# Mixture-of-experts rows planned in halves of 64: mixed blocks in two column tiles, 36 blocks for 39, and the block plan on GpSimd

## The chip, the cores and the metric

The kernel runs on one core of a Trainium2 chip. The metric is the device time of one execution in microseconds (us); lower is better. Engines are named as the profile names them: PE (TensorE, with PEld for its weight loads), DVE (VectorE), ACT (ScalarE), POOL (GpSimd) and SP (SyncE, which here only issues transfers; SPq and POOLq are the transfer queues of SP and POOL).

## What is computed

One pre-norm transformer layer on x of shape (8, 256, 256), so 2048 tokens of width 256. First comes linear attention, then a mixture of experts: each token goes to its top 2 of 8 experts, and a shared expert takes all tokens.

```python
x = x + attention(layernorm(x))          # phi(q) * cumsum(phi(k) * v), then Wo
h = layernorm(x).reshape(2048, 256)
top_logits, top_indices = top_k(h @ router_w, 2)
scores = softmax(top_logits)
for e in range(8):                       # rows of expert e only
    g, u = split(permuted @ w1[e], 2)    # 256 -> 2 x 512
    out_e = (silu(g) * u) @ w2[e]        # 512 -> 256
shared = (silu(h @ w_gate) * (h @ w_up)) @ w_down
x = x + sum(out * scores) + shared
```

The 4096 (token, expert) rows are routed by the data, so how many rows each expert has is known only while the kernel runs.

## The kernel before

Products are made in float16 with a high and a low part, as three products (high by high, low by high, high by low). Two stages follow one another:

1. **Dense stage** (steps `i` of 256 tokens): attention, router and shared expert. Meanwhile SP streams the experts' weights into `stage`, ACT makes their high part (`expert_hi`, line 935) and DVE their low part (`expert_lo`, line 1265) in `we` and `wd`. POOL computes small normalisation terms and writes each token's row, by indirect transfers, to its slot in the DRAM tensor `x_rows` (`to_rows`, line 512), where each expert has its own region of `CAP` rows.
2. **Routed stage** (blocks `b` of 128 rows of one expert). With P = 128 the number of blocks must hold for any routing: NBLK = (4096 + 8 * 127) // 128 = 39, though the data may need fewer. For block `b`, SP loads and transposes its rows (`load_rows`, lines 370 and 371) into `xg` and `meta`, PE makes gate and up (`expert_up`, banks bG and bU), ACT the silu (line 908), DVE `ab` (line 1209), ACT the high part (line 1052), DVE the low part (line 1483). PE transposes the high part (`turn_high`, line 782, bank bK), SP the low part (`turn_low`, line 379), and PE makes the down product (`expert_down`, bank bV or bQ). ACT scales it (line 1067) and POOL adds it to the output with an indirect transfer (`scatter`, line 574). The order on PE is up half 0 of `b`, `turn_high(b-1)`, up half 1 of `b`, `expert_down(b-2)`.

Between the stages stands the **block plan** (lines 1432 to 1475, on DVE): from the counts per expert it works out `blk_expert` (the expert of each block) and `blk_row` (its first row in `x_rows`). PE and SP read these into registers. Both wait for the semaphore `bexp_done`. On PE that wait stands in front of the last piece of the shared expert:

```python
pe.wait_ge(S["bexp_done"], 1)
load_expert(0)
down(B - 1, 3)
pe.wait_ge(S["ex_lo"], 3 * E)
```

Every engine works through its own list in the written order. A chain of dependent instructions on DVE is written with a helper `then`, which raises a semaphore and waits for it. A scatter waits for the one before it when the expert changes (`hold_i`), and always for the one two before. The results lie in four buffers `ya`, so ACT's result of block b waits for the scatter of block b-4.

Of the kernel before, what the change touches and what calls it, by code (L numbers as in the profile page):

```python
# [22 lines left out]
I32 = mybir.dt.int32  # L23
# [9 lines left out]
def layer_kernel(nc, x, w_att, w_bias, w_bo, w_shared, w_expert, out):  # L33
# [12 lines left out]
    NBLK = (2 * NT * P + E * (P - 1)) // P  # L46
    NBP = NBLK + 1
# [13 lines left out]
    with ExitStack() as ctx:  # L61
# [23 lines left out]
        def router_w(w):  # L85
# [75 lines left out]
        count, nblk, bend = sb("count", [P, E]), sb("nblk", [P, E]), sb("bend", [P, E])  # L161
        cnt_i, blk_i = sb("cnt_i", [P, E], I32), sb("blk_i", [P, E], I32)
# [3 lines left out]
        by_blk = [plan[:, n * NBP:(n + 1) * NBP] for n in range(2 * E, 2 * E + 9)]  # L166
        bexp, bexp_c, boff, boff_c, last, past, pad_f, sign, score = by_blk
# [16 lines left out]
        ya = [xn[1 - n // 2][:, n % 2, :] for n in range(NY)]  # L184
# [11 lines left out]
            rt end_done padded bexp_done pad_done  # L196
            xg_in0 xg_in1 xg_in2 xg_in3 sign_done score_done dst_done ta_ps ath_done atl_in0 atl_in1 atl_in2 o_ps y_done hold_done scattered0 scattered1""".split()
# [71 lines left out]
        def down_bank(i):  # L269
            return bT if i == B - 1 else bD  # L270

# [9 lines left out]
        def _(sp):  # L281
# [81 lines left out]
            def load_rows(b):  # L363

                if b >= NX:
                    sp.wait_ge(S["u_ps"], NP * B + b - NX + 1)
                sp.reg_load(row_reg, blk_row[0:1, b:b + 1])
                at = sp.snap(row_reg, min_val=0, max_val=E * CAP)
                src = xrows[bass.ds(at, P), :]
                sp.dma_start_transpose(xg[b % NX], src[:, 0:2 * D].bitcast(F16)).then_inc(S[f"xg_in{b % NX}"], 16)  # L370
                sp.dma_start(meta[:, b, :], src[:, 2 * D:2 * D + 8]).then_inc(S[f"xg_in{b % NX}"], 16)
# [9 lines left out]
            sp.wait_ge(S["bexp_done"], 1)  # L381
# [14 lines left out]
            sp.wait_ge(S["scattered0"], 16 * (NBLK // 2 + 1))  # L396
            sp.wait_ge(S["scattered1"], 16 * (NBLK // 2))

        @block.gpsimd
        def _(pool):  # L400
# [15 lines left out]
            pool.iota(row_i[:], pattern=[[0, 1]], base=0, channel_multiplier=1).then_inc(S["const_pool"], 1)  # L416

# [105 lines left out]
            pool.wait_ge(S["const_pool"], 10)  # L523
# [4 lines left out]
            pool.wait_ge(S["float_done"], 4)  # L528
            pool.tensor_copy(taken[0][:, 0, 0, :], base_i[:]).then_inc(S["taken_done"], 1)
# [28 lines left out]

            hold_reg = pool.alloc_register("hold_reg")

            def scatter(b):
# [4 lines left out]
                if b in (1, 2):  # L566
                    pool.wait_ge(before, 16)
                elif b >= 3:
# [4 lines left out]
                pool.nop(nofuse=True)  # L573
                pool.indirect_dma_start(out_rows, bass.IndirectOffsetOnAxis(ap=dst_row[:, b:b + 1], axis=0),  # L574
                                        ya[b % NY], None, bounds_check=NT * P - 1, oob_is_err=False,
                                        compute_op=ALU.add).then_inc(S[f"scattered{b % 2}"], 16)
# [7 lines left out]
        def _(pe):  # L584
# [200 lines left out]
            def expert_up(b, e, half):  # L785

                dst, done, free = ((bG, "g_ps", "sg_done"), (bU, "u_ps", "a_done"))[half]
                if half == 0:
                    pe.wait_ge(S[f"xg_in{b % NX}"], 32 * (b // NX + 1))
                pe.wait_ge(S[free], NP * B + b)  # L790
                w = [we[:, lo, bass.ds(e, 1), :].rearrange("p o (k h n) -> p (o k) h n", k=KC, h=2) for lo in range(2)]
                x2 = xg[b % NX]
                product(pe, dst[:], lambda k: x2[:, k, :], lambda k: x2[:, KC + k, :],
                        lambda k: w[0][:, k, half, :], lambda k: w[1][:, k, half, :], KC).then_inc(S[done], 1)

            def expert_down(b, e):

                n = b % NA
                pe.wait_ge(S["ath_done"], b + 1)
# [736 lines left out]
```

## Time and profile before

| | us |
|---|---|
| median of 3 runs | 391.04 |
| lowest, highest | 389.70, 391.97 |
| the profiled execution | 391.15 |
| its span on the core | 389.4 |
| PE, DVE, ACT, POOL busy | 349.4, 232.8, 219.8, 158.4 |
| first routed block starts on PE | 213.64 |

The span is the time from the first to the last instruction that the profile records; 1.75 us of the execution lie around it. The busy times are sums over both stages. A number such as L210 is a line of the kernel; the helper that writes most matmuls has line 210, so its groups are told apart by bank (bG, bU, bV).

### The profile page before, as it was taken

The page shows a single profiled execution, that of the slowest core. Times are in us where ns is not written, and L with a number is a line of the kernel's source. Part 1 is how long each engine was busy: PE and PEld are TensorE (multiplying, and loading weights), DVE is VectorE, ACT ScalarE, POOL GpSimd, SP SyncE. Part 2 cuts the span into 40 slices and gives each one's busy share as a digit, 9 for nine tenths or more (in the row PEclk, how much of TensorE's full clock was granted, in tenths as well). Part 3 has the DMA queues.
Part 4 walks back from the last instruction along what each step waited for, and adds up shares of the span by engine and source line. Part 5 has one row for each costly group of instructions (what it writes and reads, how often), then busy time and mean ns, then how long its engine had stood idle before and what let it go on. Part 6 is the DMA issues. An engine that isn't in the chain of part 4 may idle for free.

```text
span 389.4 us, 9032 instructions
## 1 busy us (share of the span) xinstructions
PE 349.4 (90%) x2850; PEld 261.0 (67%) x2850; DVE 232.8 (60%) x564; ACT 219.8 (56%) x397; POOL 158.4 (41%) x228
## 2 busy tenths in 40 slices
PE   6967499879899898996999999999999999999961
PEld 5756387768788787885988456666666666666640
DVE  5889967667698786866779633344344343443420
ACT  3778638667586786855536444544554455455430
POOL 4723175456474554344040033433433434334341
PEclk9899799989999999999999999999999999999997
DMA  6965242265573653726556467866686768657530
GB/s 200 381 164 191 42 98 83 56 135 169 112 235 72 141 176 90 213 69 186 183 185 137 110 92 101 94 93 98 96 96 88 107 89 100 97 86 91 72 33 0
DMA packets 81756, 47.35 MB, mean 122 GB/s; under 512 B 65328, under 2 KB 76848, under 8 KB 81328
## 3 DMA queue, kind: packets, MB, share of 16 engines
q1 hardware_dynamic: 72384, 36.08, 39.5%
q0 software_dynamic: 9328, 10.69, 17.8%
q8 instruction: 26, 0.43, 0.5%
q14 instruction: 18, 0.15, 0.1%
HBM read 19.10 MB, written 12.83 MB: 82 GB/s over the span
## 4 chain that ended last, share of the span: by engine, by line
PE 57%; DVE 14%; POOL 9%; issue 7%; ACT 5%; DMA 3%; SPq 1%; POOLq 1%; DVEq 0%; ACTq 0%
PE bU L210 16%; PE bG L210 15%; PE bV L210 9%; PE bQ L210 7%; PE bD L210 3%; DMA we<-in_w_shared 3%; PE bT L210 2%; PE bK L782 2%; PE bK L210 2%; POOL x_rows L512 2%; DVE ab L1209 2%; DVE al L1214 2%; DVE st L1086 2%; POOL y L452 2%; ACT xn L893 1%
## 5 line engine op out<-in xcount | busy, mean ns | idle before, releaser
L574 POOL DMA_INDIRECT out_y<-xn,dst_row x39 | 60.6, 1554 | 122.7 <-DVE dst_row L1491 66.3
L1209 DVE SCALAR_TENSOR_TENSOR ab<-bU,sg 128x512 f32<-128x512 f32 x67 | 46.2, 689 | 78.1 <-PE bU L210 78.1
L908 ACT ACTIVATE sg<-bG 128x512 f32<-128x512 f32 x67 | 39.7, 593 | 43.1 <-PE bG L210 43.0
L210 PE MATMUL bG<-we,work 128*128 x234 | 56.9, 379 | 0.2
L210 PE MATMUL bU<-we,work 128*128 x234 | 56.9, 379 | 0.0
L1052 ACT ACTIVATE ws_h<-ab 128x512 f16<-128x512 f32 x39 | 24.6, 630 | 49.1 <-DVE ab L1209 49.1
L512 POOL DMA_INDIRECT x_rows<-rows,slot_u x32 | 34.9, 1089 | 35.2 <-DVE rows L1157 16.0
L1483 DVE TENSOR_TENSOR ws_h<-ab,ws_h 128x512 f16<-128x512 f32 x39 | 27.0, 692 | 22.4 <-ACT ws_h L1052 22.4
L210 PEld LDWEIGHTS bG<-we,work 128*128 128x128 f16 x234 | 22.9, 98 | 20.5 <-issue 1.4
L1214 DVE TENSOR_TENSOR al<-ab,ah 128x512 f16<-128x512 f32 x32 | 22.0, 688 | 21.5 <-ACT ah L915 21.4
L210 PEld LDWEIGHTS bU<-we,work 128*128 128x128 f16 x234 | 21.4, 98 | 18.5
L210 PE MATMUL bV<-wd,ws_l 128*128 x240 | 29.6, 273 | 3.7 <-issue 3.4
L915 ACT ACTIVATE ah<-ab 128x512 f16<-128x512 f32 x32 | 20.0, 625 | 22.1 <-DVE ab L1209 21.6
L210 PE MATMUL bD<-ws_h,ah 128*128 128x256 f16 x112 | 21.4, 273 | 11.7 <-DVE al L1214 10.6
L210 PE MATMUL bG<-xT,ws_h 128*128 128x256 f16 x160 | 28.2, 280 | 3.0 <-DVE ws_l L1271 2.8
L210 PEld LDWEIGHTS bV<-wd,ws_l 128*128 128x128 f16 x240 | 23.2, 98 | 11.3 <-issue 4.9
L210 PE MATMUL bU<-xT,ws_h 128*128 128x256 f16 x160 | 27.6, 275 | 0.6 <-DVE ab L1209 0.6
L210 PE MATMUL bQ<-wd,ws_l 128*128 x228 | 28.0, 273 | 0.0
L210 PEld LDWEIGHTS bQ<-wd,ws_l 128*128 128x128 f16 x228 | 22.2, 98 | 6.5
L1059 ACT ACTIVATE ws_l<-bK 128x512 f16<-128x512 f32 x39 | 23.1, 591 | 0.1
L210 PE MATMUL bD<-ws_l,ah 128*128 128x256 f16 x112 | 21.6, 275 | 0.0
L210 PE MATMUL bD<-ws_h,al 128*128 128x256 f16 x112 | 21.4, 272 | 0.0
(227 smaller groups left out, 732.1 us busy)
## 6 DMA issues: line engine op xcount, KB each, us to landing
stage<-in_w_expert SPq DMA_DIRECT2D x24, 512.0 KB, 4.5
we<-in_w_shared SPq DMA_DIRECT2D x3, 1024.0 KB, 12.4
xs<-bo POOLq DMA_DIRECT2D x8, 256.0 KB, 3.9
out_y<-xs SPq DMA_DIRECT2D x8, 256.0 KB, 2.3
xs<-in_x SPq DMA_DIRECT2D x1, 1280.0 KB, 18.1
x_rows<-we SPq DMA_DIRECT2D x9, 134.0 KB
xs<-in_x SPq DMA_DIRECT2D x3, 256.0 KB, 4.0
work<-x_rows SPq DMA_TRANSPOSE x39, 3.0
```

The lines of the kernel that those rows point to most:

```text
L210: ins = pe.matmul(dst, a(c), b(c), start=first and s == 0 and c == 0, stop=last and s == 2 and c == n - 1, skip_group_check=lone)
L452: pool.tensor_tensor(y0[1][:], ve[1][:], minus_half[:], ALU.pow).then_inc(S["pow2"], 1)
L512: pool.indirect_dma_start(xrows, bass.IndirectOffsetOnAxis(ap=slot_u[q][:, k, t:t + 1], axis=0), rows2[q][:, t, :].bitcast(U16), None).the ...
L574: pool.indirect_dma_start(out_rows, bass.IndirectOffsetOnAxis(ap=dst_row[:, b:b + 1], axis=0), ya[b % NY], None, bounds_check=NT * P - 1, ...
L782: ins = pe.matmul(bK[:, c * P:(c + 1) * P], ar_h[b % NA][:, c * P:(c + 1) * P], ident16[:], start=True, stop=True)
L908: act.activation(sg[q][:], src[:], ACT.Silu, scale=1.0 / WS).then_inc(S["sg_done"], 1)
L915: act.activation(ah[f][:], ab[f % 2][:], ACT.Copy).then_inc(S["ah_done"], 1)
L1052: act.activation(ar_h[n], ab[b % 2][:], ACT.Copy).then_inc(S["ah_done"], 1)
L1059: act.activation(aT_h[n].rearrange("p c l -> p (c l)"), bK[:], ACT.Copy).then_inc(S["ath_done"], 1)
L1209: dve.scalar_tensor_tensor(out=ab[q][:], in0=src[:], scalar=1.0 / WS, in1=sg[q][:], op0=ALU.mult, op1=ALU.mult).then_inc(S["a_done"], 1)
L1214: dve.tensor_tensor(al[f][:], ab[f % 2][:], ah[f][:], ALU.subtract).then_inc(S["al_done"], 1)
L1483: dve.tensor_tensor(ar_l[n], ab[b % 2][:], ar_h[n], ALU.subtract).then_inc(S["al_done"], 1)
```

## The change

Rows are counted in halves of 64. An expert with an odd number of halves has one half left over; two such halves, of two experts, share one **mixed block**. Four fixed places are kept for mixed blocks: MIXED = 5, 13, 21, 29. The number of blocks that holds for any routing falls to 36.

- In a mixed block PE multiplies rows 0 to 63 with one expert's weights and rows 64 to 127 with another's. Each matmul of a block becomes two, each with 64 columns of weights (the rows), which write partitions 0 to 63 and 64 to 127 of the bank. In the built program they carry tile size 128x64 at column 0 and column 64; all others carry 128x128.
- The second expert's weights are copied ahead of time by DVE into the tile `stage` (`lend_weights`, 6 copies of 128x1024 float16 for each mixed block, spread over the five blocks in front of it).
- SP loads a mixed block with two transposes and two small loads; POOL scatters it with two indirect transfers, one behind the other.
- The block plan moves from DVE to POOL, behind the last `to_rows`; it now also has to place the mixed blocks. DVE keeps 9 short instructions of it. SP waits for `row_done`, PE for `bexp_done`; both are raised by POOL.
- `ya` lies in `xs` instead of `xn`. POOL has 9 more short instructions at the start of the kernel.

Core of the diff:

```diff
-    NBLK = (2 * NT * P + E * (P - 1)) // P
-    NBP = NBLK + 1
+    HALF = P // 2
+    NPAIR = E // 2
+    NBLK = ((2 * NT * P + E * (HALF - 1)) // HALF + 1) // 2
+    NBP = NBLK + 2
+    GAP = 8
+    MIX0 = 5
+    MIXED = [MIX0 + GAP * q for q in range(NPAIR)]
...
-            sp.wait_ge(S["bexp_done"], 1)
+            sp.wait_ge(S["row_done"], 1)
...
+            pool.wait_ge(S["plan_in"], 3)
+            then(pool.tensor_scalar(gap[:], nblk, -float(P), float(CAP), ALU.mult, ALU.add), wait=False)
...
+            then(pool.tensor_tensor(bcmp, wide(full, E), over(bend[:], NBP), ALU.subtract), wait=False)
+            then(pool.tensor_tensor(lmul[:, :, 0:4], lmul[:, :, 0:4], lmul[:, :, 4:8], ALU.add))
+            then(pool.tensor_scalar(bcmp, bcmp, 0.0, None, ALU.is_ge))
...
+            then(pool.tensor_tensor(bmul, bcmp, over(gap[:], NBP), ALU.mult), wait=False)
...
+            then(pool.tensor_copy(blk_row[:], boff))
+            pool.tensor_scalar(mixed_of(blk_row), mixed_of(boff), upper[:, 2:3], None, ALU.add).then_inc(S["row_done"], 1)
+            then(pool.tensor_tensor(bmul[:, :, 0:4], bcmp[:, :, 0:4], bcmp[:, :, 4:8], ALU.add))
+            then(pool.tensor_tensor(bmul[:, :, 0:2], bmul[:, :, 0:2], bmul[:, :, 2:4], ALU.add))
+            then(pool.tensor_tensor(bexp, bmul[:, :, 0], bmul[:, :, 1], ALU.add))
+            then(pool.tensor_scalar(bexp_c, bexp, float(E - 1), None, ALU.min))
+            pool.tensor_copy(blk_expert[:], bexp_c).then_inc(S["bexp_done"], 1)
...
-                if b in (1, 2):
-                    pool.wait_ge(before, 16)
+                if b in (1, 2) or b in MIXED or b - 1 in MIXED:
+                    pool.wait_ge(before, 16 * ((b + 1) // 2))
...
+                if b in MIXED and half == 0:
+                    pe.wait_ge(S["lent"], 6 * MIXED.index(b) + 4)
+                x2, n = xg[b % NX], P // two(b)
+                for s, (hi, lo) in enumerate(((0, 0), (1, 0), (0, 1))):
+                    for k in range(KC):
+                        for t in range(two(b)):
+                            ins = pe.matmul(dst[t * n:(t + 1) * n, :], x2[:, hi * KC + k, t * n:(t + 1) * n], w[t][lo][:, k, half, :],
+                                            start=s == 0 and k == 0, stop=s == 2 and k == KC - 1, skip_group_check=True)
...
-            dve.wait_ge(S["pad_done"], 1)
+            dve.wait_ge(S["pad_done"], 2)
             shared_out(B - 1)
...
+                for q in range(NPAIR):
+                    if MIXED[q] - 5 <= b < MIXED[q]:
+                        for k in ((0,), (1,), (2,), (3,), (4, 5))[b - MIXED[q] + 5]:
+                            lend_weights(q, k)
```

How the instructions stand on the engines, in three places.

**PE, gate product of block 5.** Before, it is six matmuls of 128 columns of weights, with register instructions (ISA) for the expert's address between them, and then the transposes of block 4:

```order
L210 ISA [waits sg_done,xg_in1]
L210 MATMUL bG<-we,work 128x512
L210 ISA
L210 MATMUL bG<-we,work 128x512 x3
L210 ISA
L210 MATMUL bG<-we,work 128x512
L210 ISA
L210 MATMUL bG<-we,work 128x512
L782 MATMUL bK<-ident,ws_h 128x128 [waits ath_done,ah_done]
L782 MATMUL bK<-ident,ws_h 128x128 x3
```

The same place now, from the wait for the lent weights on, with the end of the twelve matmuls and the transposes:

```order
L930 ISA [waits lent]
L930 MATMUL bG<-we,work 64x512
L930 MATMUL bG<-stage,work 64x512
L930 ISA
L930 MATMUL bG<-we,work 64x512
L930 MATMUL bG<-stage,work 64x512
L930 MATMUL bG<-we,work 64x512
L930 MATMUL bG<-stage,work 64x512
L930 MATMUL bG<-we,work 64x512
L930 MATMUL bG<-stage,work 64x512
```

Each matmul has become two with half the columns of weights and the same 512 streamed columns. The transposes behind them still have 128 columns, so the tile size changes there and back.

**DVE, behind the last step's counts.** Before, the plan's 18 instructions up to `blk_row` stand between `base` and the next `ab` (`work` holds the plan's intermediate tiles); its last part:

```order
L1441 TENSOR_SCALAR gap<-nblk 128x8
L1442 TENSOR_TENSOR work<-iota_f,bend 128x320 [waits rt]
L1443 TENSOR_TENSOR work<-work,gap 128x320 [waits rt]
L1444 TENSOR_REDUCE work<-work 128x40
L1445 TENSOR_REDUCE work<-work 128x40 [waits rt]
L1446 TENSOR_SCALAR work<-work 128x40
L1447 CAST blk_expert<-work 128x40 [waits rt]
L1449 SCALAR_TENSOR_TENSOR work<-iota_f,work 128x40
L1450 TENSOR_SCALAR work<-work 128x40 [waits rt]
L1451 CAST blk_row<-work 128x40 [waits rt]
L1209 SCALAR_TENSOR_TENSOR ab<-bU,sg 128x512 [waits u_ps,sg_done]
```

Now nine instructions are left there:

```order
L1575 COPY base<-bR 128x8 [waits rank_ps]
L1578 CAST end_i<-base 128x8 [waits float_done,base_done]
L1579 SCALAR_TENSOR_TENSOR cnt_i<-base 128x8
L1581 TENSOR_TENSOR hop<-base 128x7 [waits rt]
L1582 TENSOR_SCALAR halves_i<-cnt_i 128x8
L1583 TENSOR_SCALAR halves_i<-cnt_i 128x8
L1584 CAST halves<-halves_i 128x2x8 [waits rt]
L1585 SCALAR_TENSOR_TENSOR lend<-ones,halves 128x8 [waits rt]
L1586 SCALAR_TENSOR_TENSOR bend<-ones,halves 128x8
L1354 SCALAR_TENSOR_TENSOR ab<-bU,sg 128x512 [waits u_ps,sg_done]
L1359 TENSOR_TENSOR al<-ab,ah 128x512 [waits ah_done]
L1410 SCALAR_TENSOR_TENSOR we<-stage,we 128x1024 [waits ex_hi]
```

The work on `ab`, `al` and the weights' low parts moves up by that much.

**POOL, behind the last rows of the dense stage.** Before, the scatter of block 0 follows at once. Now the plan does; its start is:

```order
L553 DMA x_rows<-rows,slot_u 17536x536 x3
L621 TENSOR_SCALAR gap<-halves 128x8 [waits plan_in]
L622 TENSOR_SCALAR first_row<-halves,upper 128x1
L623 TENSOR_SCALAR paired<-half_f,lend 128x4
L624 TENSOR_TENSOR half_at<-half_f,paired 128x4 [waits pt]
L625 TENSOR_TENSOR shift_by<-paired 128x2
L626 TENSOR_TENSOR pairs<-shift_by 128x1 [waits pt]
L627 TENSOR_TENSOR work<-half_at,lend 128x32
```

It runs on so, line by line of the plan: 33 instructions up to `row_done` (line 654), 5 more to `bexp_done` (line 659), 11 more to the second `pad_done` (line 670) and 4 to `hold_done`. POOL's plan thus begins behind the four indirect transfers of the last step.

## Rows read from the trace of the kernel before

**Rows 1.** The page: busy us, share of the span and count of each engine.

```profile
PE 349.4 (90%) x2850; PEld 261.0 (67%) x2850; DVE 232.8 (60%) x564; ACT 219.8 (56%) x397; POOL 158.4 (41%) x228
```

**Rows 2.** One stretch of routed stage: us, busy per engine, clock, DMA share, GB/s.

```profile
300.00:340.00 40.00, 40.00 (x271) 24.72 (x270) 16.17 (x49) 20.26 (x40) 15.45 (x11) 1.00 0.71 99
```

**Rows 3.** The chain that ended last, one block: start us, us, what.

```profile
327.49 1.31 PE bQ L210 x12
328.80 1.29 PE bG L210 x6
330.10 0.22 PE bK L782 x4
330.32 1.29 PE bU L210 x6
```

**Rows 4.** The page, a group: busy us, mean ns of one.

```profile
L210 PEld LDWEIGHTS bG<-we,work 128*128 128x128 f16 x234 | 22.9, 98 | 20.5 <-issue 1.4
```

**Rows 5.** Timeline of PE at the border of the stages: start us, us, what.

```profile
212.07 0.39 PE L210 MATMUL bT<-ws_h,ah 128*128 128x256 f16 x2
212.30 0.38 PE L210 MATMUL bT<-ws_h,al 128*128 128x256 f16 x2
...
213.64 1.47 PE L210 MATMUL bG<-we,work 128*128 x6
```

**Rows 6.** Timeline of POOL in a dense step, short dependent instructions.

```profile
172.01 1.10 POOL L459 TENSOR_TENSOR nt<-y 128x2 f32<-128x2 f32 x1
173.19 0.20 POOL L461 TENSOR_TENSOR nu<-nt,ve 128x2 f32<-128x2 f32 x1
173.47 0.19 POOL L463 TENSOR_SCALAR nw<-nu 128x2 f32<-128x2 f32 x1
...
174.22 0.20 POOL L469 TENSOR_TENSOR shift<-mv,neg 128x2 f32<-128x2 f32 x1
174.37 0.25 POOL L499 TENSOR_TENSOR taken<-taken,oh 128x32 f16<-128x32 f16 x1
```

**Rows 7.** Timeline of DVE in the same stretch.

```profile
171.84 1.22 DVE L1265 SCALAR_TENSOR_TENSOR wd<-stage,wd 128x1024 f16<-128x1024 f32 x1
```

**Rows 8.** Timeline of POOL: the last rows written in the dense stage.

```profile
199.34 0.97 POOL L512 DMA_INDIRECT x_rows<-rows,slot_u  x1 [0.30 <-issue]
```

**Rows 9.** Groups of DVE from 200.3 to 213.3 us: busy us, mean ns.

```profile
L1265 DVE SCALAR_TENSOR_TENSOR we<-stage,we 128x1024 f16<-128x1024 f32 x3 | 3.7, 1219 | 0.3 <-ACT we L935 0.3
L1214 DVE TENSOR_TENSOR al<-ab,ah 128x512 f16<-128x512 f32 x4 | 2.8, 688 | 1.4 <-ACT ah L915 1.4
L1265 DVE SCALAR_TENSOR_TENSOR wd<-stage,wd 128x1024 f16<-128x1024 f32 x2 | 2.5, 1226 | 0.3 <-ACT wd L935 0.3
```

**Rows 10.** Timeline of SP's queue: first rows of block 0.

```profile
207.74 1.23 SPq L370 DMA_TRANSPOSE work<-x_rows  x1
209.18 0.41 SPq L371 DMA_DIRECT2D meta<-x_rows  x1
```

**Rows 11.** DMA issues: count, KB each, median us to landing.

```profile
meta<-x_rows SPq DMA_DIRECT2D x39, 2.0 KB, 2.4
```

**Rows 12.** Two stretches of 2 us in the dense stage (columns of Rows 2).

```profile
44.00:46.00 2.00, 0.00 (x0) 0.00 (x0) 1.97 (x5) 1.91 (x6) 0.00 (x0) 0.50 0.33 66
48.00:50.00 2.00, 2.00 (x13) 1.43 (x11) 0.40 (x1) 0.60 (x1) 0.78 (x1) 0.58 1.01 160
```

**Rows 13.** Timeline of POOL: a scatter, and the next, which waits for it.

```profile
293.02 1.55 POOL L574 DMA_INDIRECT out_y<-xn,dst_row  x1 [2.58 <-DVE dst_row L1491]
299.01 1.55 POOL L574 DMA_INDIRECT out_y<-xn,dst_row  x1 [4.43 <-DMA out_y<-xn,dst_row]
```

**Rows 14.** Timeline of SP's queue in the routed stage, one block.

```profile
329.85 1.20 SPq L379 DMA_TRANSPOSE ws_l<-ws_h  x1
332.06 1.20 SPq L370 DMA_TRANSPOSE work<-x_rows  x1
```

**Rows 15.** Timeline of DVE in the routed stage, with its idle time in front.

```profile
331.72 0.69 DVE L1209 SCALAR_TENSOR_TENSOR ab<-bU,sg 128x512 f32<-128x512 f32 x1 [1.85 <-PE bU L210]
```

More of the change, by code:

```diff
@@ L195, in layer_kernel @@
             tok_done tanh_done t_done rows_clear saved0 saved1
[L196 to L197 removed]
+            rt pt plan_in end_done padded bexp_done pad_done
+            xg_in0 xg_in1 xg_in2 xg_in3 sign_done score_done dst_done ta_ps ath_done atl_in0 atl_in1 atl_in2 o_ps y_done hold_done row_done lent halves_out scattered0 scattered1""".split()
         S = {n: sem(n) for n in names}
@@ L270, in down_bank, with rows_in, mixed_of, over @@
             return bT if i == B - 1 else bD
+        def rows_in(b):
+            return S[f"xg_in{b % NX}"], sum(64 if n in MIXED else 32 for n in range(b % NX, b + 1, NX))
+        def mixed_of(a):
+            return a[:, 0:GAP * NPAIR].rearrange("p (q r) -> p q r", r=GAP)[:, :, MIX0]
+        def over(a, m):
+            return a.rearrange("p (o m) -> p o m", o=1).to_broadcast((P, m, a.shape[1]))
+        def wide(a, m):
+            return a.rearrange("p (m o) -> p m o", o=1).to_broadcast((P, a.shape[1], m))
         def xs_of(i):
@@ L557, in _, with then @@
             to_rows(B - 1)
+            n_pt = [0]
+            def then(ins, wait=True):
+                n_pt[0] += 1
+                ins.then_inc(S["pt"], 1)
+                if wait:
+                    pool.wait_ge(S["pt"], n_pt[0])
+            mixed = bcmp[:, 0:GAP * NPAIR, :].rearrange("p (q r) e -> p q r e", r=GAP)[:, :, MIX0, :]
+            pool.wait_ge(S["plan_in"], 3)
+            then(pool.tensor_scalar(gap[:], nblk, -float(P), float(CAP), ALU.mult, ALU.add), wait=False)
+            then(pool.tensor_scalar(first_row[:], nblk[:, 0:1], upper[:, 1:2], None, ALU.add), wait=False)
@@ new lines, in _ @@
+            then(pool.tensor_scalar(paired[:], half_f[:, 0, :], lend[:, E - 1:E], None, ALU.is_lt))
+            then(pool.tensor_tensor(half_at[:], half_f[:, 1, :], paired[:], ALU.mult), wait=False)
+            then(pool.tensor_tensor(shift_by[:, 0:2], paired[:, 0:2], paired[:, 2:4], ALU.add))
+            then(pool.tensor_tensor(pairs[:], shift_by[:, 0:1], shift_by[:, 1:2], ALU.add), wait=False)
+            then(pool.tensor_tensor(lcmp, wide(half_at[:], E), over(lend[:], NPAIR), ALU.subtract))
@@ new lines, in _ @@
+            then(pool.tensor_copy(full, iota_f[:]), wait=False)
+            then(pool.tensor_scalar(lcmp, lcmp, 0.0, None, ALU.is_ge), wait=False)
+            then(pool.tensor_scalar(passed[:], iota_f[:, 1:NPAIR + 1], pairs[:, 0:1], None, ALU.min))
+            later = full[:, MIX0 + 1:MIX0 + 1 + GAP * NPAIR].rearrange("p (q r) -> p q r", r=GAP)
+            then(pool.tensor_tensor(later, later, wide(passed[:], GAP), ALU.subtract), wait=False)
+            then(pool.tensor_scalar(half_pad[:, :, 0], paired[:], float(-P), None, ALU.mult))
@@ new lines, in _ @@
+            then(pool.tensor_tensor(mixed_of(full), mixed_of(full), half_pad[:, :, 0], ALU.add))
+            then(pool.tensor_tensor(lmul[:], lcmp, over(halves[:, 1, 1:E + 1], NPAIR), ALU.mult))
+            then(pool.tensor_tensor(bcmp, wide(full, E), over(bend[:], NBP), ALU.subtract), wait=False)
+            then(pool.tensor_tensor(lmul[:, :, 0:4], lmul[:, :, 0:4], lmul[:, :, 4:8], ALU.add))
+            then(pool.tensor_scalar(bcmp, bcmp, 0.0, None, ALU.is_ge))
+            then(pool.tensor_tensor(mixed, mixed, lcmp, ALU.add), wait=False)
@@ new lines, in _ @@
+            then(pool.tensor_scalar(past, boff, row_f[:, 0:1], base[:, 0:1], ALU.add, ALU.subtract))
+            then(pool.tensor_tensor(pad_f, past, last, ALU.subtract))
+            then(pool.tensor_scalar(past, pad_f, 0.0, float(BIG), ALU.is_ge, ALU.mult))
+            pool.tensor_copy(pad_i[:], past).then_inc(S["pad_done"], 1)
+            for t in range(2):
+                then(pool.tensor_scalar(half_pad[:, :, t], mixed_of(past), other[:, t:t + 1], None, ALU.max), wait=t == 1)
+            pool.tensor_copy(half_pad_i[:], half_pad[:]).then_inc(S["pad_done"], 1)
```

203 lines of the change are left out of this document (137 added, 66 removed).

## The prediction

> **What bounds the kernel now.** I read the page first: PE is busy for 90% of the span, the other engines for 41 to 60% [rows 1]. That is an average over two stages, so next came stretches. From 300 to 340 us PE is busy for all of 40.00 us at the full clock (2.4 GHz), with DVE at 16.17, ACT at 20.26 and POOL at 15.45 [rows 2]. The chain that ended last runs there over PE alone: the reader should see four pieces without a gap, 1.31 (down), 1.29 (gate), 0.22 (transposes) and 1.29 us (up), and the next down begins where the last ends [rows 3]. Together 4.11 us; with rounding a block costs 4.12 us. So the routed stage is bound by PE, and a block more or less is worth 4.12 us.
>
> Last I read the border of the stages. PE begins its last shared piece at 212.07 and block 0 at 213.64, straight behind it [rows 5]. SP issues block 0's rows at 207.74, behind other transfers of its queue [rows 10]. They need 1.44 us to the issue of `meta` and 2.4 us for it to land [rows 10, 11], so they are there at 207.74 + 1.44 + 2.4 = 211.6. The slack over PE is 213.64 - 211.6 = 2.0 us. That is all the room for a later plan on SP's side.
>
> **The blocks.** Three blocks fewer: 3 * 4.12 = -12.4 us, with the ramp at the start and the tail at the end of the stage as before.
>
> **The mixed blocks, if the two tiles run side by side.** Each matmul becomes two which stream the same number of columns. If the two stream at once, a mixed block streams for 4.12 us like any other. The trace before has no such pair, so the cost is bounded: at least nothing, at most each matmul in full. In full, 1.29 + 1.29 + 1.31 = 3.89 us more per mixed block [rows 3], 15.6 us in all. The two use different columns of the array and write different partitions of the bank, so neither needs anything that the other holds; I take side by side, and keep the other end as a rival.
>
> The tile size also changes six times for a mixed block (around its gate, its up and its down product), 24 times in all. If PE must finish what it runs before it changes, each change costs what a matmul still takes after the next one could start: a pair of matmuls lasts 0.39 us while pairs start 0.23 us apart [rows 5], so 0.16 us. Bounds: 0 and 24 * 0.16 = 3.9 us. I take 3.9, since the rows show that this tail exists and is only hidden by the next matmul of the same kind.
>
> The Trainium skill (TensorEngine Tiling (Array Packing), section Tiling Modes, Key Properties) says of this that a change of the tiling mode, not merely of the tile, drains TensorE, while different tiles load weights and multiply in parallel. By both halves of that rule the sum comes out as I take it; without the drain it would be 3.9 us lower. No row here shows either.
>
> **The plan on POOL.** This is the term that needs most working.
> - *Start.* POOL's last transfer of rows begins at 199.34 and takes 0.97 us, so the plan begins at 200.3 [rows 8]. DVE's nine instructions are done by then: they stand right behind the slots for which POOL's four transfers wait.
> - *Undisturbed.* 33 instructions up to `row_done`. Short dependent ones start 0.28 us apart, independent ones 0.15 [rows 6]. 18 are waited for and 15 not: 18 * 0.28 + 15 * 0.15 = 7.3 us. Size: 2 elements take 0.20 us, 32 take 0.25 [rows 6], so 1.7 ns for each element; the 33 have 1608 elements per partition together: 2.7 us. Sum 10.0, hence 210.3.
> - *Disturbed by DVE.* POOL's 128x2 product took 1.10 us instead of 0.20 when DVE's product of two SBUF tiles ran from 171.84 to 173.06; it ended with it, at 173.11 [rows 6, 7]. So a POOL instruction that starts under such a DVE instruction ends only after it. While the plan runs, DVE has five of these of 1.22 us and four of 0.69 [rows 9], the first of the four now ahead of the plan, since DVE is rid of most of its own. Each lets one POOL instruction through, of some 0.25 us: 5 * 0.97 + 3 * 0.44 = 6.2 us lost at most. The first of the five falls mostly ahead of 200.3, and in some cases POOL is first and DVE waits; I take 4.8. `row_done` is then at 215.1 (bounds 210.3 and 216.5).
> - *Behind it.* Five more instructions (342 elements, 5 * 0.28 + 0.6 = 2.0 us) give `bexp_done` at 217.1. On PE `down(B - 1, 3)` is queued behind that wait. PE is idle from 212.07 to 217.2. In the dense stage the granted clock fell to half (1.2 GHz) in such a stretch: idle from 44 to 46 us at 0.50, and from 48 to 50, busy throughout, still 0.58 [rows 12]. I take it that the first 3.5 us of work run at half speed. The last shared piece then takes about 2 * 1.31 + 0.2 = 2.8 us, until 220.0. SP issues block 0's rows at 215.1 + 0.5 (a register load), and they land 3.84 us later, at 219.4. Block 0 starts at 220.1 for 213.64, +6.5 us, and 0.7 us of it still run at half speed, +0.4. Sum +6.9. Without any disturbance: `bexp_done` 212.3, rows there at 214.6, block 0 at about 214.7, so +1.1 and no halved clock. With all 6.2 us lost: +8.3.
> - *What else waits there.* `pad_done` comes 11 instructions later, near 220.6; `shared_out` and the first `ab` need it, but that `ab` is due only at 220.1 + 2.6, so it is covered by up to 2 us. `hold_done` is far ahead of the first scatter.
>
> The Trainium skill (GPSIMD Engine Reference, section Elementwise side-by-side cycle accounting) gives about 2.6 cycles at 1.2 GHz, 2.2 ns, for each element of a two-input operation on GpSimd, against 1.7 ns by my rows. As an estimate by that page the plan would take 0.8 us longer, and the kernel too. The rows decide here, but they reach only to 32 elements and the plan has 304.
>
> **What I cost at nothing.** *DVE's copies*, 24 of 128x1024. The nearest row is the product of the same size, 1.22 us [rows 9]; DVE is idle for 1.85 us in front of each `ab` [rows 15]. The cover fails only where two stand in one block (2.4 us), by some 0.6 us, and there ACT and PE have room for it; without cover at most 4 * 0.6 = 2.4 us. *SP's second transpose* and small load for a mixed block, about 2.1 us of queue. SP starts the next load 1.0 us after it has finished issuing (329.85 + 1.20 against 332.06, the wait for PE and a register load among it) [rows 14], so it falls behind and recovers over the eight blocks between mixed ones; rows are loaded four blocks ahead and the low parts' transpose has over 2 us until `expert_down`. Uncovered: 4 * 2.1 = 8.4 us. *POOL's nine instructions at the start*, at most 9 * 0.28 = 2.5 us, lie in the wait for the first weights. *The two scatters in a row*: see the rivals.
>
> **Sum.** -12.4 + 3.9 + 6.9 = -1.6 us. The profiled execution took 391.15, so 389.55; it stands 0.1 above the median, so for the median 391.04 - 1.6 = 389.4 us. A measurement of this kernel can tell about 0.5%, 2 us. This case, with its own range of 386 to 392.5 us, has a chance of 0.50.
>
> **Rivals.**
> - *The plan or the drains are cheap* (0.28). POOL meets fewer DVE instructions than counted, or changing the tile size costs little. With an undisturbed plan and drains: -12.4 + 3.9 + 1.1 = -7.4, 383.6 us. With the plan as late as forecast but no drain: 385.5. With both away: -11.3, 379.7. For it speaks that the border's term rests on a lock read from single rows; against, that DVE is busy with such instructions for over 8 of the 13 us [rows 9].
> - *The pair costs more than one matmul* (0.13, slower). Its place is the mixed block on PE. One after the other it is +15.6: -12.4 + 15.6 + 6.9 = +10.1, 401 us (no drain is seen then). It decides from 24% of that price on: -1.6 + 0.24 * 15.6 = +2.1. A milder form is that weight loads are no longer hidden. In the trace they are hidden, 24.72 us of PEld under 40.00 us of PE [rows 2], at 98 ns each [rows 4]. With 192 loads of half the columns, 49 ns each, laid open: +9.4, 398.8 us. The Trainium skill (TensorE: Matmul & The Clock Gate, Part 3) says that a weight load overlaps running matmuls only where the row group differs, and both tiles of a pair have the same one. By that rule the milder form happens; but full tiles share a row group too, and their loads are hidden, so it has 0.05 of the 0.13.
> - *The scatters fall behind* (0.09, a little slower). A scatter that waits for the one before starts 5.99 us after it [rows 13]. Around a mixed block four stand in such a row: the one behind it starts 3 * 6.0 = 18.0 us after the one ahead of it, for 2 * 4.12. ACT needs the buffer of block b-1 for b+3, of b for b+4 at 20.6 us and of b+1 for b+5 at 24.7, and they are free at 6, 18 and 24. So it is hidden with 0.7 us to spare. At 7 us for each it is not: 28 - 24.7 = 3.3 us for each of four, +13, less what the ramp of buffers takes up; I put 394 to 400 on it.
>
> **How the numbers follow.** The range goes from an undisturbed plan with part of the drains gone, 382 us, up to the weight loads laid open, 399 us. It leaves out about 0.06 below, and above it the serial pair (0.08) and a little of the scatters' case (0.02). Below 389.1 lie two fifths of the forecast's case (0.21) and the cheap one (0.28): 0.49. Above 393.0 lie the two slow rivals (0.22) and the upper end of the forecast's case (0.05): 0.27. The rest, 0.24, is within 0.5%.
>
> **What would show it.** In the routed stage twelve matmuls of 64 columns for a gate product in about 1.3 us with 0.1 to 0.2 us before and behind (2.6 us: the pair is serial). POOL instructions of the plan with 0.7 to 1.2 us beside DVE's low parts, `row_done` near 215, PE idle near 212 to 217 with a granted clock of 0.5 behind it, block 0 near 220. 36 blocks at 4.12 us elsewhere. Wrong would be: block 0 at 215 or below, a mixed block over 5.2 us, or PE waiting for ACT five blocks behind a mixed one.

## The result: slower, 404.35 for 391.38 us

| | before | changed kernel |
|---|---|---|
| median of 4 runs on one chip | 391.38 us | 404.35 us |
| lowest and highest | 389.7, 391.97 | 401.91, 409.32 |
| ratio, 95% interval | | 1.0318, 1.0237 to 1.0398 |
| profiled execution, its span | 391.15, 389.4 | 409.32, 407.5 |

The longest of the changed kernel's four, 409.32 us, counts as a slow execution, so the ratio leaves it out (the other three have a median of 402.68 us), and since it is the profiled one, 5 us over the median, its stretches add up to more than the median's loss.

From the page of the changed kernel, PE's busy time (before: [rows 1]) and the granted clock in 40 slices:

```profile
PE 350.4 (86%) x2862; PEld 257.1 (63%) x2862; DVE 232.4 (57%) x556; ACT 215.1 (53%) x385; POOL 186.1 (46%) x291
...
PEclk9798989999999999999996888999999699999986
```

Windows of the changed kernel, with the columns of [rows 2]:

```profile
300.00:340.00 40.00, 36.96 (x250) 21.75 (x249) 15.56 (x46) 17.26 (x33) 14.30 (x10) 0.91 0.63 80
340.00:380.00 40.00, 38.73 (x279) 23.24 (x278) 17.39 (x51) 19.32 (x38) 15.76 (x10) 1.00 0.66 84
```

PE was busy for all 40.00 us of the first stretch before. Now 3 us are missing, and the mean clock is 0.91.

**The border.** PE's timeline:

```profile
212.60 0.38 PE L230 MATMUL bT<-ws_l,ah 128*128 128x256 f16 x2
221.24 0.59 PE L230 MATMUL bT<-ws_h,ah 128*128 128x256 f16 x2 [8.26 <-POOL blk_expert L659]
...
223.75 2.77 PE L930 MATMUL bG<-we,work 128*128 x6
226.31 1.85 PE L930 MATMUL bU<-we,work 128*128 x6
228.00 1.46 PE L930 MATMUL bG<-we,work 128*128 x6
```

Block 0 starts at 223.75 for 213.64 [rows 5]. The last shared piece takes 2.5 us and block 0's gate product 2.77 us for 1.47: half clock, until about 227. POOL's timeline says why it is so late (first, second, a large, a held, the last of `row_done`, the last of `bexp_done`):

```profile
201.33 0.21 POOL L621 TENSOR_SCALAR gap<-halves 128x8 f32<-128x8 f32 x1
201.63 1.38 POOL L622 TENSOR_SCALAR first_row<-halves,upper 128x1 f32<-128x1 f32 x1
...
207.54 0.71 POOL L636 TENSOR_TENSOR work<-work,bend 128x304 f32<-128x304 f32 x1
...
211.09 1.27 POOL L640 TENSOR_TENSOR lmul<-lmul 128x8 f32<-128x8 f32 x1
...
218.47 0.32 POOL L654 TENSOR_SCALAR blk_row<-work,upper 128x4 int32<-128x4 f32 x1
...
220.44 0.22 POOL L659 CAST blk_expert<-work 128x38 int32<-128x38 f32 x1
```

`row_done` comes at 218.8 and `bexp_done` at 220.7. Eight elements that took 1.27 us were held by DVE.

**The routed stage.** The group of the down products has a wait that was next to nothing before: `PE bQ L948 <- DMA ws_l<-ws_h`, 9.9 us in 5 waits; before, it came to 0.2 us. The first is at block 1. SP's queue there (start, time to issue), and PE:

```profile
231.45 1.22 SPq L418 DMA_TRANSPOSE ws_l<-ws_h  x1
233.32 1.17 SPq L409 DMA_TRANSPOSE work<-x_rows  x1
234.68 0.60 SPq L410 DMA_DIRECT2D meta<-x_rows  x1
236.16 1.19 SPq L409 DMA_TRANSPOSE work<-x_rows  x1
237.56 0.47 SPq L410 DMA_DIRECT2D meta<-x_rows  x1
238.08 1.27 SPq L418 DMA_TRANSPOSE ws_l<-ws_h  x1
```

```profile
237.25 1.46 PE L930 MATMUL bU<-we,work 128*128 x6
242.20 2.74 PE L948 MATMUL bQ<-wd,ws_l 128*128 x12 [3.49 <-DMA ws_l<-ws_h]
```

DVE had block 1's low parts ready at 232.87 + 0.69 = 233.6. Their transpose stood behind both half loads of block 5 until 238.08 and landed at 242.2. PE waited for 3.49 us and then ran at half clock (2.74 for 1.53 us), as the window of the 4 us behind the gap shows (the column behind the engines is the granted clock):

```profile
242.00:246.00 4.00, 3.80 (x15) 2.28 (x16) 0.00 (x0) 0.47 (x1) 0.00 (x0) 0.50 0.43 81
```

The same happens at 279.10 (0.44 us), 316.68 (3.04, half clock again) and 354.27 (0.83): always in front of the down product of the block that comes four before a mixed one. The fifth, 2.05 us, is in the tail, where PE waited for 2.99 before.

Each of the four gaps is a sum. The low parts wait in SP's queue from the moment DVE has them ready, then they land (from SP's issue to the start of PE's product), and PE waits for what exceeds the room, the time from ready until PE could have begun:

| block | wait in SP's queue, us | landing | room | gap of PE |
|---|---|---|---|---|
| 1 | 4.52 | 4.12 | 5.15 | 3.49 |
| 9 | 3.20 | 3.31 | 6.07 | 0.44 |
| 17 | 3.61 | 5.50 | 6.07 | 3.04 |
| 25 | 3.59 | 3.31 | 6.07 | 0.83 |

The queue waits of blocks 17 and 25 are the same; their gaps differ because the landing took 5.5 us in one and 3.3 in the other. The issue and PE's product at block 17:

```profile
311.18 1.24 SPq L418 DMA_TRANSPOSE ws_l<-ws_h  x1
316.68 2.74 PE L948 MATMUL bQ<-wd,ws_l 128*128 x12 [3.04 <-DMA ws_l<-ws_h]
```

**A mixed block itself.** PE's timeline across the end of its gate product:

```profile
251.24 0.38 PE L930 MATMUL bG<-we,work 128*64 x1
251.25 0.38 PE L930 MATMUL bG<-stage,work 128*64 128x512 f16 x1
251.46 0.38 PE L930 MATMUL bG<-we,work 128*64 x1
251.46 0.38 PE L930 MATMUL bG<-stage,work 128*64 128x512 f16 x1
251.77 0.40 PE L910 MATMUL bK<-ident,ws_h 128*128 128x128 f16 x4
252.10 0.40 PE L930 MATMUL bU<-we,work 128*64 x1
```

Both tiles start together, and pairs follow every 0.22 us, as full matmuls do. Behind the last pair 251.77 - 251.46 - 0.22 = 0.09 us are lost, about 0.1 at each change of tile size.

### The profile page after: what moved, and what is told of

Read it like the earlier page. It is cut to its first block and busy times, and to the rows that moved or that the text cites. A ratio compares the mean times of both kernels' runs of the same rounds, so it can differ in the third digit from the quotient of the medians.

```text
span 407.5 us, 8954 instructions
## 1 busy us (share of the span) xinstructions
PE 350.4 (86%) x2862; PEld 257.1 (63%) x2862; DVE 232.4 (57%) x556; ACT 215.1 (53%) x385; POOL 186.1 (46%) x291
## 5 line engine op out<-in xcount | busy, mean ns | idle before, releaser
L702 POOL DMA_INDIRECT out_y<-xs,dst_row x32 | 50.3, 1573 | 86.0 <-DMA out_y<-xs,dst_row 35.1
L930 PE MATMUL bG<-we,work 128*128 (+1 forms) x216 | 56.6, 401 | 0.5 <-issue 0.3
L930 PE MATMUL bU<-we,work 128*128 (+1 forms) x216 | 53.2, 383 | 0.0
L948 PE MATMUL bQ<-wd,ws_l 128*128 (+1 forms) x216 | 30.6, 298 | 9.9 <-DMA ws_l<-ws_h 9.9
L930 PEld LDWEIGHTS bG<-we,work 128*128 128x128 f16 (+1 forms) x216 | 22.0, 104 | 22.4 <-issue 6.2
L948 PEld LDWEIGHTS bQ<-wd,ws_l 128*128 128x128 f16 (+1 forms) x216 | 22.4, 107 | 19.8 <-issue 15.5
L930 PEld LDWEIGHTS bU<-we,work 128*128 128x128 f16 (+1 forms) x216 | 20.1, 100 | 18.1 <-issue 1.3
L948 PE MATMUL bV<-wd,ws_l 128*128 x216 | 26.6, 273 | 0.1
L948 PEld LDWEIGHTS bV<-wd,ws_l 128*128 128x128 f16 x216 | 20.9, 98 | 6.7 <-issue 0.9
L697 POOL DMA_INDIRECT out_y<-xs,half_dst x8 | 12.4, 1544 | 26.4 <-DMA out_y<-xs,dst_row 14.5
```

What stands on the lines that cost most here:

```text
L930: ins = pe.matmul(dst[t * n:(t + 1) * n, :], x2[:, hi * KC + k, t * n:(t + 1) * n], w[t][lo][:, k, half, :], start=s == 0 and k == 0, stop ...
L948: ins = pe.matmul(dst[t * m:(t + 1) * m, :], a[:, c, t * m:(t + 1) * m], w[t][:, c, lo, :], start=s == 0 and c == 0, stop=s == 2 and c == ...
```

## The experiments

Each is compared with the kernel before on its own chip. Ratios are to that.

**1. `e1_before36`: the blocks alone.** The kernel before with

```diff
-    NBLK = (2 * NT * P + E * (P - 1)) // P
-    NBP = NBLK + 1
+    NBLK = 36
+    NBP = NBLK + 2
```

> The kernel before with 36 blocks for 39 and nothing else of the change (this batch of tokens needs 35, so every row is still computed). Both theories take a block at 4.12 us, so 3 * 4.12 = 12.4 us less: 391.04 - 12.4 = 378.7 us. If a fixed tail or the ramps take part of it, up to 381. Above 384 would say that the term for the blocks was too large, and that the loss of 25.7 us against the sum (404.35 where 391.04 - 12.4 = 378.6) is smaller than I think.

Measured 380.49 us, ratio 0.9703 (0.9631 to 0.9775), that is 11.6 us less on the 391.04 of before. From block 0's gate product to the last down product it is 368.92 - 216.04 = 152.9 us, where it was 379.19 - 213.64 = 165.6: 12.7 us for three blocks. The term holds.

**2. `e2_plain`: plan on POOL, no mixed block.**

```diff
-    MIXED = [MIX0 + GAP * q for q in range(NPAIR)]
+    MIXED, WHOLE = [], [MIX0 + GAP * q for q in range(NPAIR)]
```

(For the blocks in `WHOLE`, DVE takes the padding of the lower half.)

> The changed kernel with its plan on POOL and 36 blocks, but the four mixed blocks run as plain ones: one load, one matmul for each pair, one scatter, no weight copies on DVE. It leaves out the rows of the upper halves of the mixed blocks. My theory: what the mixed blocks lay on SP, PE and POOL costs 13 to 17 us (gaps of PE of 3.49, 0.44, 3.04 and 0.83 us at the low parts' transposes, the half clock behind them, 24 drains of 0.09 us, the scatters at the end), and the late plan 10 us: 391.04 - 12.4 + 10.1 = 388.7 us. Rival: the gaps come from POOL's late plan and a DMA system that is still catching up, not from the mixed blocks: then this kernel keeps gaps and stands at 395 to 402 us.

387.97 us, ratio 0.9889 (0.9852 to 0.9926). The plan on POOL costs 388.0 - 380.5 = 7.5 us. What mixed blocks do costs the rest, 404.35 - 388.0 = 16.4. The rival (a late plan makes the gaps) falls. One gap of 0.62 us in front of a down product is left in the routed stage, at 254.61, for low parts that took 4.95 us to land: without any second load the room is already small.

**3. `e3_turn_first`: SP's order, only at mixed blocks.**

```diff
+                if b + NX in MIXED:
+                    turn_low(b)
                 if b + NX < NBLK:
                     load_rows(b + NX)
-                turn_low(b)
+                if b + NX not in MIXED:
+                    turn_low(b)
```

> The changed kernel with one step moved on SP: where the block four ahead is a mixed one, the transpose of the low parts of block b is issued before the two half loads instead of behind them. My theory (SP issues it too late): the gaps of PE of 3.49, 0.44, 3.04 and 0.83 us in front of the down product go, 7.8 us, and with the two long ones some 1.3 us each of work at half clock: 404.35 - 10.4 = 394 us, range 392 to 396. Rival (the transfer itself is slow there, because four transfers of rows share the DMA engines with scatters): the transpose is issued earlier but lands as late, or the loads of the mixed blocks come late instead; 401 to 405 us, with gaps of the same size.

408.64 us, ratio 1.0402 (1.0325 to 1.0479): my expectation was wrong. PE's timeline shows that the gap moved one block on and grew:

```profile
246.30 2.69 PE L951 MATMUL bV<-wd,ws_l 128*128 x12 [4.68 <-DMA ws_l<-ws_h]
```

The transpose of block 2 now stood behind the two half loads (234.23 and 237.08) and the load of block 6 (240.44), until 242.31. So it isn't one given transpose that is late, but the one that stands behind the two half loads.

**4. `e4_short_low`: DVE's long instructions beside the plan cut.**

```diff
                 (hi, src), (lo, _) = expert_part(p, 0), expert_part(p, 1)
+                if p >= part_of_step(B, 2):
+                    hi, src, lo = hi[:, 0:1], src[:, 0:1], lo[:, 0:1]
```

> The changed kernel with DVE's five low parts of expert weights beside the plan cut from 1024 to 1 or 256 elements per partition (their other elements are zero, filled one step earlier). It leaves out most of the low part of five weight pieces. Only POOL's plan is read. If DVE's long instructions of two SBUF tiles hold POOL off, the plan's 17.5 us (201.33 to 218.8) fall to about 12 or 13. If POOL's instructions are by themselves this slow, they stay at 16 to 17.5 us. My prediction had 10.0 us undisturbed and 4.8 us of hold.

One run, 397.9 us. POOL's timeline, first and last instruction up to `row_done`:

```profile
201.52 0.20 POOL L621 TENSOR_SCALAR gap<-halves 128x8 f32<-128x8 f32 x1
...
213.98 0.31 POOL L654 TENSOR_SCALAR blk_row<-work,upper 128x4 int32<-128x4 f32 x1
```

12.8 us for 17.5: DVE's five long instructions hold POOL off for 4.7 us. Of the other 12.8 us some are still hold, by the DVE instructions of 0.69 us that were left. Two that start under one of these last far longer than others of their size (0.58 us for 4 elements, where 0.21 is seen in the changed kernel, and 0.75 for 38, where 0.26 is):

```profile
204.80 0.58 POOL L634 TENSOR_TENSOR work<-work,half_pad 128x4 f32<-128x4 f32 x1
...
212.10 0.75 POOL L650 TENSOR_TENSOR work<-work 128x38 f32<-128x38 f32 x1
```

With a third (line 641, 1.17 us where line 636 with as many elements takes 0.78) that is 1.3 us, so POOL's own time is about 11.5 us and the whole hold about 6.0.

**5 to 7. SP's order for every block, the plan on DVE, and both.** The order:

```diff
+                turn_low(b)
                 if b + NX < NBLK:
                     load_rows(b + NX)
-                turn_low(b)
```

The plan on DVE is the same computation; rows are added up with `tensor_reduce` and multiply-adds made one instruction, so that it has 25 instructions up to `bexp_done`, in pieces between DVE's other work. Its core:

```diff
             swiglu(n, 0)
+            plan(0)
             act_lo(j, 0)
             expert_lo(part_of_step(B, 2))
             swiglu(n + 1, 1, bV)
+            plan(1)
             act_lo(j, 1)
             expert_lo(part_of_step(B, 3))
+            plan(2)
```

> The changed kernel with SP's order turned for every block: the low parts of block b are transposed first, then the rows of block b + 4 are loaded. The run that turned it only at the mixed blocks moved the gap by one block (4.68 us at the transpose of block 2, which stood behind two half loads and the load of block 6) and was slower, 408.6. My theory now: SP's queue is nearly full (two transposes and a small load take some 3.7 of 4.12 us), a mixed load puts it back by 2.9 us, and what stands behind must be the thing that can wait. Rows have some 10 us of room, low parts 2 to 4. So the gaps of 3.49, 0.44, 3.04 and 0.83 us and the half clock behind two of them go: 404.35 - 10.4 = 394 us, range 392 to 397. Rival: the transposes themselves take long to land beside four row transfers and scatters: gaps stay, 400 to 406.

> The changed kernel with the same plan computed on DVE in three pieces between its other work (25 instructions up to the block's expert, since DVE adds along a row and multiplies and adds in one instruction each), the padding behind its last low part; POOL has none of it. DVE had about 4 us idle between 198 and 212; the plan needs some 5. My theory: block 0 starts near 216 for 223.75, PE is idle for 2 to 3 us and its clock is not halved for long: 404.35 - 8.5 = 396 us, range 394 to 398. Rival: DVE's work is itself the bound up to the last low part (213.21 before), so its plan pushes the shared pieces and the low parts by all of 5 us, PE is short of silu products too, and little is won: 400 to 404. The gaps at the low parts' transposes stay in both.

> Both of the other two edits: plan on DVE, low parts ahead of rows on SP. If they are independent the gains add: 404.35 - 10.4 - 8.5 = 385.5 us, range 383 to 388, so below before's 391. Rival: the scatters at the end (the chain that ended last in the changed kernel) take over, with 13 scatters and four extra ones that wait for the one before, and the sum is short by 3 to 6 us: 388 to 392.

| | us | ratio, 95% interval |
|---|---|---|
| order alone | 398.88 | 1.0169, 1.0096 to 1.0241 |
| plan on DVE alone | 394.07 | 1.0063, 1.0028 to 1.0098 |
| both | 390.28 | 0.9964, 0.9928 to 1.0001 |

The plan is worth a little more than I expected (10.3 us for 8.5). The order is worth about half, 5.5 for 10.4, and 398.88 lies above my range. Both together came out at 390.28 where I expected 385.5, in the range of the rival, but by the trace not for its reason, the scatters at the end: six gaps of PE at the low parts, 7.2 us together, are left. In the kernel with both, block 0 starts at 215.02, with 0.85 us of idle PE before the last shared piece. SP, and PE at the first of the six gaps:

```profile
225.73 1.17 SPq L409 DMA_TRANSPOSE work<-x_rows  x1
...
228.57 2.04 SPq L409 DMA_TRANSPOSE work<-x_rows  x1
...
231.35 1.27 SPq L418 DMA_TRANSPOSE ws_l<-ws_h  x1
```

```profile
234.26 1.53 PE L883 MATMUL bV<-wd,ws_l 128*128 x12 [1.64 <-DMA ws_l<-ws_h]
```

**8. `e8_gap7`: mixed blocks at 5, 12, 19, 26** (`GAP = 7`, on top of both).

> As the run with both edits, with the mixed blocks at 5, 12, 19 and 26 instead of 5, 13, 21 and 29, so that six scatters more lie between the last mixed block's two and the end. If the tail is bound by scatters behind block 29: 1 to 3 us less, 383 to 384. If PE and its last transposes bound the end: the same, 385.5. Rival: seven blocks are too few for SP or DVE's copies to recover in, and it is 2 to 4 us slower.

387.88 us, ratio 0.9906 (0.987 to 0.9941): 2.4 us under the one before it, with intervals that overlap. That scatters of a late mixed block lengthen the tail is not shown by it: in the profiled executions of runs 7 and 8 it is as long, 10.4 (389.8 - 379.38) and 10.3 us (389.2 - 378.94) from the last down product to the end of the span.

**9. `e9_spread`: the half loads in two steps**, on top of that.

```diff
+            todo = [(b, (t,)) for b in range(NX, NBLK) for t in range(2 if b in MIXED else 1)]
             for b in range(NBLK):
                 turn_low(b)
-                if b + NX < NBLK:
-                    load_rows(b + NX)
+                for _ in range(2 if b in MIXED else 1):
+                    if todo and todo[0][0] <= b + NX:
+                        load_rows(*todo.pop(0))
```

> As the run with the mixed blocks at 5, 12, 19 and 26 (387.88, with gaps of PE at the low parts' transposes of 2.03, 2.18, 0.76 and 1.18 us), with one step moved on SP: the two halves of a mixed block's rows are loaded in two steps of the loop, each behind a transpose of low parts; the loads behind them come one step later until the step of the mixed block itself, which loads two. So no transpose of low parts stands behind more than one load until then. My theory (what counts is how long a transpose of low parts stands in SP's queue): most of 6.15 us of gaps goes, 387.9 - 5 = 383 us, range 381 to 385. Rival: rows loaded one step later arrive too late, or the landing time of 3 to 5 us is the cause and not the queue: 387 to 391.

386.04 us, ratio 0.9853 (0.9799 to 0.9906), the lowest of the kernels with mixed blocks (its interval overlaps that of run 8) and faster than the kernel before, but only 1.8 us of the 5 that I expected. It still stands above the 380.49 us of run 1, which has 36 blocks and nothing else of the change. The gap behind block 5's load is gone. Others are left, among them a new kind, 1.11 us in front of block 12 (and 0.94 at block 26), for rows that now come late:

```profile
265.59 0.40 PE L867 MATMUL bG<-we,work 128*64 x1 [1.11 <-DMA meta<-x_rows]
```

Another, of 1.68 us, has the cause that the rival names, the landing:

```profile
354.89 1.53 PE L885 MATMUL bQ<-wd,ws_l 128*128 x12 [1.68 <-DMA ws_l<-ws_h]
```

These low parts were ready at 347.15 and issued at 349.26, so they waited in the queue for 2.1 us, and took 5.6 to land. So the order deals out the queue's lack of room, and the landing time, which no run changes alone, decides with it whether PE waits. The rival is not refuted.

**10 and 11. One load for a mixed block, two loads for a plain one.** The sharpest pair: take the suspect away, and put it back alone.

```diff
-                got, parts = S[f"xg_in{b % NX}"], 2 if b in MIXED else 1
+                got, parts = S[f"xg_in{b % NX}"], 1
```

```diff
-                got, parts = S[f"xg_in{b % NX}"], 2 if b in MIXED else 1
+                got, parts = S[f"xg_in{b % NX}"], 2 if b in WHOLE else 1
```

> The changed kernel with the rows of a mixed block loaded in one piece, as a plain block's; everything else of a mixed block stays (two column tiles, two scatters in a row, the copies on DVE). The upper half of block 5, the only one which this batch fills with another expert's rows, is left out for that. My theory (the second load on SP is what costs): 404.35 less the gaps of 7.8 us and the half clock behind them of 2.6 us, 394 us, range 391 to 396; it should stand 4 us or so above the plain one (388.0: drains 2.2, tail 1.7). Rival (the tiles, the scatters or the copies cost most of the 16.4 us between the two): 399 to 404.

> The kernel with four plain blocks in place of the mixed ones (388.0), and of all that a mixed block does only this added back: its rows are loaded as two halves of 64. It leaves out the rows of the upper half of block 5. My theory: the same gaps of PE as in the changed kernel come back, at blocks 1, 9, 17 and 25, 7.8 us and 2.6 us of half clock: 398 us, range 395 to 401. Rival (mixed blocks cost through tiles, scatters or copies): 388 to 391.

With one load: 390.96 us, ratio 1.0004 (0.9977 to 1.0031), just below my range, and PE waits for low parts only in the tail. Plain blocks with two loads: 397.84 us, ratio 1.0159 (1.0105 to 1.0213), as expected, and gaps are back without a tile, a second scatter or a copy. They are not the same four, though: large ones stand at blocks 1 and 25, a smaller one, 0.65 us, at block 0, and at blocks 9 and 17 PE waits for 0.24 us at most. PE's timeline of that one:

```profile
240.95 2.65 PE L947 MATMUL bQ<-wd,ws_l 128*128 x12 [3.23 <-DMA ws_l<-ws_h]
...
310.83 1.53 PE L947 MATMUL bQ<-wd,ws_l 128*128 x12 [0.24 <-issue]
...
347.49 1.53 PE L947 MATMUL bQ<-wd,ws_l 128*128 x12 [1.82 <-DMA ws_l<-ws_h]
```

At block 17 the low parts waited in SP's queue for 3.5 us, as long as in the changed kernel, but landed within 2.8 us instead of 5.5, and the gap is 0.24 us instead of 3.04. At block 25 they landed in 4.7 us.

The rivals (tiles, scatters, copies) fall as the main cause: together they cost 391.0 - 388.0 = 3.0 us by the medians, 4.5 by the ratios.

**12. `e12_down_first`: PE's last shared piece ahead of its wait**, on the kernel of run 2.

```diff
+            down(B - 1, 3)
             pe.wait_ge(S["bexp_done"], 1)
             load_expert(0)
-            down(B - 1, 3)
```

> The kernel with four plain blocks in place of the mixed ones (388.0), with PE's last shared piece put ahead of the wait for the blocks' experts, behind which it was queued. Seen there: PE idle for 8.25 us until 219.67, the piece at half clock until 222.18, block 0 from 222.18 (its gate product 2.77 us), rows there by about 221.4. My theory: block 0 can start at 221.4, 0.8 us earlier, but now the work at half clock is all block 0's, some 4 us of it where the shared piece took 2.5 of it before, which gives 0.8 to 1.3 us back: the same, 387 to 388.5. Rival (what stands behind the wait costs its time): the 2.5 us at the border shrink to what the rows need, 386.5 to 387.

387.85 us (ratio 0.9905, 0.9873 to 0.9938) for 387.97, no change. PE's timeline:

```profile
221.58 2.74 PE L929 MATMUL bG<-we,work 128*128 x6 [7.46 <-DMA meta<-x_rows]
224.11 2.13 PE L929 MATMUL bU<-we,work 128*128 x6
226.08 1.46 PE L929 MATMUL bG<-we,work 128*128 x6
```

Block 0 starts at 221.58 for 222.18, but now all of the half-clock work is its own, and block 1's gate product starts at 226.08 for 226.30. What was queued behind the wait cost next to nothing: it took the half clock on itself.

## Why the prediction was wrong

- **Blocks, -12.4:** right. 11.6 us by the ratio, 12.7 by the traces.
- **The pair side by side:** right, and with it that the rival of 398.8 us, weight loads laid open, did not come. The Trainium skill (TensorE: Matmul & The Clock Gate, Part 3) lets a load overlap only where the row group differs; here both tiles share one and pairs still follow every 0.22 us, so the trace disagrees with that sentence for this case. The same part of the Trainium skill also allows it for a load into the background weight buffer; which buffer a load went to, no trace shows.
- **Drains, +3.9:** the right mechanism, sized too large (and 24 * 0.16 is 3.8). The tail is 0.1 us instead of 0.16, so 24 * 0.1 = 2.4 us. The Trainium skill (TensorEngine Tiling (Array Packing), Key Properties) says that a change of mode drains TensorE; the trace agrees, with 0.1 us.
- **The plan on POOL, +6.9:** 7.5 by runs 1 and 2, near enough, but by luck, since its parts were off. The hold by DVE was about 6.0 us for 4.8, near the bound of 6.2: 4.7 from the five long instructions and 1.3 from the short ones (run 4). POOL's own time was about 11.5 us for 10.0. The price of an element held (304 elements took 0.71 us, and 0.20 + 304 * 0.0017 is 0.72), but all short ones were priced at 0.20 us, and a `tensor_scalar` of one to four elements takes up to 0.31; 12 of the 33 are `tensor_scalar`. With a start one us later, `row_done` came at 218.8 for 215.1. Block 0 came 10.1 us later in the profiled execution for 6.5, and half clock lasted for 5.9 us of work instead of 3.5. The time shows less of it, as block 0 can start later with nothing changed ahead of it (run 1: 216.04 for 213.64); from run 1 to run 2 it is 222.18 - 216.04 = 6.1 us, and 1.5 more of half clock behind it.
- **The step that failed** stands under "What I cost at nothing": *SP's second transpose* and small load "about 2.1 us of queue", of which SP "falls behind and recovers over the eight blocks", "Uncovered: 4*2.1 = 8.4 us". I had the price and gave it no chance. It is 9.9 us alone (run 11 against run 2; 10.6 by the ratios) and 13.4 beside the other parts (404.35 - 390.96; 12.3 by the ratios). Three things in it were wrong:
  - A second load takes 2.8 us (233.32 to 236.16), since a register load stands between the two.
  - SP has little to recover with: from one transpose of low parts to the next it was 238.08 - 231.45 = 6.63 us with two half loads, so 3.8 of 4.12 us with one, and I had read the 1.0 us in front of a load [rows 14] as free, though 0.65 of it is there even when SP is behind. At 0.3 us free in a block, working off 2.8 us would take nine, an estimate. The trace bears it out in part: from 280 to 308 us each load starts 0.65 to 0.76 us after the issue in front of it, so SP is behind all the way to the next mixed load, but after the first gap it waits for PE again within one block, 1.3 us in front of the load at 240.63, since PE had stood still as well.
  - What counts is the transpose right behind the two loads, and there "over 2 us until `expert_down`" was not enough. The low parts of block 1 were ready at 233.6 and needed by 238.7, when PE began to wait (242.20 - 3.49); they took 4.1 us to land, which leaves 1.0 us of room in the queue for a wait of 4.5. The landing, of which the prediction says nothing there, took 2.8 to 5.5 us at such places; why it varies is open.

  Behind each of the two long gaps PE runs for over 5 us at half clock and loses 2.6 and 2.9 us (in run 11 it is 1.7 behind the first gap), which I had counted at the border only.
- **DVE's copies** are hidden, and cost 0.42 us each for 1.22.
- **The scatters in a row** did not hold up ACT for more than 0.9 us once. From the last down product to the end of the span it was 13.1 us (407.5 - 394.41) for 10.2, 1.2 of it half clock. That the scatters lengthen it is not shown: in run 3, with the same scatters, it is 11.1 us.
- **The range**, 382 to 399, ended below the result since its upper end came from PE and POOL alone.

The ledger by the medians: 391.4, less 10.9 for three blocks (380.5), plus 7.5 for the plan (388.0), plus 3.0 for the tiles, scatters and copies (391.0) or plus 9.9 for the second loads (397.8), and 404.35 with both. Of the 16.4 us from 388.0 to 404.35 the two make 12.9, and 3.5 are left over. By the ratios, each run against the kernel before on its own chip, it is -11.6, +7.3, +4.5 and +10.6 us, and of 16.8 us only 1.7 are left over, with an uncertainty of some 4 us by the intervals. So it is not shown that the two cost more together than each alone.

## What to carry to other kernels

Before a step is put on a queue, add up what that queue does in one period: this one was busy for 3.8 us of 4.1, and what stood behind an extra 2.8 us was late by that much. Then ask of each extra transfer which waiter stands behind it, not when it is itself due, and give that waiter room for its own landing time at its longest (here 5.5 us, not 2.8). An order of the queue alone won back about half of the loss in run 5 and made it worse in run 3. And a long gap of PE costs twice, once for itself (3.49 us) and once for the half clock behind it (2.6 us).

## What was not expected of the hardware

- Copying 128x1024 f16 from SBUF to SBUF takes DVE 0.42 us, where the three-operand f32 form of that size took 1.22 [rows 9].
- A transfer of half the rows is not cheaper to issue: 1.17 to 1.19 us for 64 rows, 1.19 to 1.23 for 128, where nothing held it up.
- The same transpose of low parts (`ws_l`) landed within 2.8 us of its issue in one run and 5.5 in another, at the same block. Why is open.
- Half clock (1.2 GHz) ended at about the same time in runs 2 and 12, 225.3 and 225.4 us by PE's products, though PE's work began at 219.67 in the one and, after 7.46 us of idle time, at 221.58 in the other. Why is open.
